# Chunked reads at the loop's opening, more steps inside the loop, and the second group's output projection moved into its last quarter

## The chip, the cores and the metric

The kernel runs on one core of a Trainium2 chip. The metric is the device time of one execution in microseconds (us). The time before is the median of three runs, 2076.06 us (2075.85 to 2076.21).

## The reference

A language-model tower on 8 sequences of 256 tokens, 2048 tokens in all, width D = 192. First comes a stack of four layers (12 heads of 16, each token attends to keys at a distance of up to 64). Then come a channel attention, a mixture of four experts, a full self-attention with 12 heads over each sequence, and a mixture of eight experts. Cut to what matters here:

```python
for l in range(4):                       # LAYERS
    q, k, v = heads(h @ Wq[l] + bq[l]), heads(h @ Wk[l] + bk[l]), heads(h @ Wv[l] + bv[l])
    a = band_attention(q, k, v, mask)    # softmax(q k^T / 4) v, |distance| <= 64
    h = layer_norm(h + a @ Wo[l] + bo[l], ln1_s[l], ln1_b[l])
    f = gelu(h @ W1[l] + b1[l])          # 192 -> 768
    h = layer_norm(h + f @ W2[l] + b2[l], ln2_s[l], ln2_b[l])
```

The later full self-attention uses the same attention code, without a band.

## The kernel before, in words

**Tiles and groups.** The 2048 tokens are 16 tiles of 128 tokens (NT), in four groups g of four tiles (GT). A group holds two of the eight sequences, called batches b in the code. The layer loop runs four times (`Fori`); the later full attention calls the same functions a fifth time. Each engine has its own instruction list, in an order that is written out by hand, and the lists meet at semaphores.

**Opening of a layer.** A tile of `h` is turned by TensorE (`pe_transpose`, L396) and split into a high and a low part by ScalarE (`act_split`, L603) and VectorE (`dve_split`, L707, L708). This is called a tile here. A group's projection has seven items: three chunks of 128 columns for q and k together (64 of each, so four heads; `pe_features`, L414 to L418; ScalarE reads the bank with `act_qk`, L621) and four v tiles (`pe_tokens`, L424 to L428; `dve_v`, L727). Each q or k value is cut into three bf16 pieces: for group 0 by VectorE (`dve_pieces`, L716 to L718), for the others by GpSimd (`pool_pieces`, L946 to L949). GpSimd cuts v as well (`pool_v`, L983 to L986). The pieces go through memory to get their layout: the SP queue writes them to `qk_rows` (L960, six DMAs a group, with runs of 1,024 bytes), waits for all six, and reads each batch back with 12 DMAs (L969) into `qx` and `kx`, in runs of 512 bytes, since a head's 16 rows lie apart from the next head's. The opening handles tiles 0 to 15, all seven items of group 0 and the three chunks of group 1. Then the loop's first scores wait for the 12 reads of batch 0.

**Loop.** A layer's 96 pairs of heads p (24 a group, 12 a batch) run as a software pipeline. For each p, TensorE makes the scores of pair p (L501 mask, L504), the value products of pair p-5 (L533 to L535) and the transposes of the probabilities of pair p-3 (L515). VectorE takes maxima (L735) and makes `ptl` (L741). ScalarE makes two exponentials (L638) and `pth` (L649). Between the pairs stand single steps which all use one PSUM bank, `BM[0]`: the items of the next group, one every third pair (`next_projection`; group 1 has only its four v tiles there, at p = 1, 4, 7, 10; groups 2 and 3 have chunks at the first three places of their 24 pairs and v tiles at the next four), and, from p = 70 in every second pair, `late_step`: four tiles of the attention output turned and split ("att", tiles 0 to 3), four output projections ("out", tiles 0 to 3, five matmuls and one addition on VectorE), then att of tiles 4 to 7.

**Tail.** After the loop TensorE projects tiles 4 to 7 (`pe_out_group(1)`), turns group 0 of the normed `h` (`pe_turn(2, 0)`) and runs the hidden layer (`pe_hidden`, L414 to L418 and L596). The turns of later groups and two more output groups stand at fixed places in it (`under`). VectorE's order is in `dve_tail`: the residual and statistics of group 1, then turn(2, 0), then for each group affine, residual, statistics and turn(2, g+1). GpSimd makes the reciprocal root (`pool_rstd`, L895, L896).

Of the kernel before, what the change touches and what calls it, by code (L numbers as in the profile page):

```python
# [24 lines left out]
ALU = mybir.AluOpType  # L25
# [7 lines left out]
B, S, D, FF = 8, 256, 192, 768  # L33
# [14 lines left out]
SLOTS = ((0, 0), (0, 1), (1, 0), (1, 1), (0, 2), (2, 0))  # L48
ROWS = DH * len(SLOTS)
ITEMS = 7  # L50
AHEAD = 3
LATE = 70
# [63 lines left out]
def build_tower(nc, a, out, stop=None):  # L116
    ctx = ExitStack()
    with ctx:
# [151 lines left out]
        pieces_out = sig("pieces_out", per=96 * NG, base=0)  # L270
        qk_in = [sig(f"qk_in_{j}", per=16 * 12 * len(range(j, B, 3)), base=0) for j in range(3)]
# [70 lines left out]
        qk_rows = [nc.dram_tensor(f"qk_rows_{j}", (2, 3, D, GW), BF16, kind="Internal").ap() for j in range(2)]  # L342
# [21 lines left out]
        def late_step(p):  # L364

            i = (p - LATE) // 2
            if p < LATE or (p - LATE) % 2 or i >= 3 * GT:
                return None
            return ("att", i) if i < GT else ("out", i - GT) if i < 2 * GT else ("att", i - GT)

        def pe_late(pe, it, p, w):

            if late_step(p) is None:
                return
            kind, t = late_step(p)
            if kind == "att":
                if t == 0:
                    pe.wait_ge(vf_ready.sem, vf_ready.at(it, 4 * NG))
                if t == GT:
                    pe.wait_ge(o_read.sem, o_read.at(it, GT))  # L380
                pe_transpose(pe, it, turned(1, t), t, xn, att_ready, it, t + 1, True)
            else:
                if t == 0:
                    pe.wait_ge(wb_ready.sem, wb_ready.at(it, 1))
                    pe.wait_ge(xx_ready.sem, xx_ready.at(it, turned(1, GT - 1) + 1))
                else:
                    pe.wait_ge(o_read.sem, o_read.at(it, t))
                pe_tokens(bank[BM[0]][:, 0:D], w, 0, D, t).then_inc(o_done.sem, 1)
# [41 lines left out]
        def projection_at(g, i):  # L430

            n = ITEMS * g + i
            return bank[BM[n % 3 if n < ITEMS + AHEAD else 0]]

        def pe_qkv(pe, it, g, i, wa):


            n = ITEMS * g + i
            proj_read(pe, it, n - (3 if n < ITEMS + AHEAD else 1))
# [7 lines left out]
        def proj_read(pe, it, n):  # L447

            g, i = n // ITEMS, n % ITEMS
            if n < 0:  # L450
                return
            if i < 3:
# [1560 lines left out]
```

## Time and profile before

| | |
|---|---|
| Median of three runs | 2076.06 us |
| Profiled execution, its own time | 2083.07 us |
| Its span, first to last instruction | 2081.2 us |
| Mean granted TensorE clock | 0.877 |
| Busy: PE, DVE, ACT, POOL | 75%, 65%, 53%, 34% of the span |
| Pairs of the second layer, first to last maximum | 151.3 us (390.76 to 542.04) |
| From its last maximum to the third layer's first | 143.69 us |

Busy shares are a mean over stages with different limits, so the stages are read apart, by stretches of the span. All times of one instruction are counted from the span's start. The chain of waits tells what ended an idle stretch; a wait for several semaphores is put down to the last. The kernel does the same in each of the four layers, and most rows below are of the second (from 352 us on).

### The profile page before, as it was taken

To read this page: it belongs to the slowest core of one execution; us is meant where nothing else is said; L and a number is where in the kernel's file an instruction comes from. 1 tells how busy PE (TensorE), PEld (TensorE's weight loads), DVE (VectorE), ACT (ScalarE), POOL (GpSimd) and SP (SyncE) were. 2 spreads that over 40 slices of the span, in tenths; PEclk is the share of its full clock that TensorE was granted. 3 is DMA by queue.
4 is the path that set the end of the run, shared out by engine and by line. 5 is a ranking of instruction groups with operands and counts; after the bars stand their busy time and mean duration, and the time that the engine had idled before them with its cause. 6 is when DMAs were issued, how large, how long until landed. Compare 5 with 4: busy or idle time off the path is not lost.

```text
span 2081.2 us, 47737 instructions
## 1 busy us (share of the span) xinstructions
PE 1567.8 (75%) x14634; PEld 1321.3 (63%) x14634; DVE 1350.8 (65%) x3622; ACT 1106.3 (53%) x3351; POOL 710.9 (34%) x989
## 2 busy tenths in 40 slices
PE   0589787798787798786898865975936887649993
PEld 0467666677576677674776663845925666449992
DVE  5688865688865789755889654243446998454444
ACT  0389732699523799324897312323515996225551
POOL 5644123534132552124441231013444340034541
PEclk9899888899898999898998885877967999669996
DMA  5868100876001955005681000015727660147775
GB/s 138 163 111 99 25 1 2 151 95 87 2 1 36 146 86 68 1 1 98 113 99 27 1 7 6 1 41 173 231 89 103 88 86 2 41 150 227 238 233 165
DMA packets 191387, 178.61 MB, mean 86 GB/s; under 512 B 23056, under 2 KB 176208, under 8 KB 190992
## 3 DMA queue, kind: packets, MB, share of 16 engines
q1 hardware_dynamic: 183824, 158.19, 39.2%
q0 software_dynamic: 7296, 17.18, 2.4%
q8 instruction: 129, 2.11, 0.5%
q14 instruction: 138, 1.13, 0.2%
HBM read 132.96 MB, written 42.34 MB: 84 GB/s over the span
## 4 chain that ended last, share of the span: by engine, by line
PE 49%; DVE 23%; issue 11%; ACT 6%; DMA 5%; POOL 2%; SPq 2%; DVEq 1%; ACTq 0%; POOLq 0%
PE bank L1313 6%; DVE ptl L741 6%; PE bank L596 5%; PE bank L515 4%; DVE neg_max L735 3%; PE bank L533 2%; PE bank L396 2%; ACT pth L649 2%; DMA kx<-qk_rows 2%; PE bank L414 2%; PE bank L1299 2%; PE bank L504 2%; ACT prob L638 2%; PE bank L417 2%; PE bank L416 2%
## 5 line engine op out<-in xcount | busy, mean ns | idle before, releaser
L638 ACT ACTIVATE prob<-bank,neg_max 128x192 f32<-128x192 f32 (+1 forms) x960 | 416.9, 438 | 71.5 <-DVE neg_max L735 40.9
L741 DVE TENSOR_TENSOR ptl<-bank,pth 128x512 f16<-128x512 f32 x480 | 329.3, 686 | 24.9 <-ACT pth L649 20.5
L735 DVE TENSOR_REDUCE neg_max<-bank 128x2 f32<-128x384 f32 (+1 forms) x480 | 274.1, 571 | 95.5 <-PE bank L504 92.4
L515 PE MATMUL bank<-ident,prob 128*128 128x128 f32 x1920 | 311.6, 286 | 0.0
L649 ACT ACTIVATE pth<-bank 128x512 f16<-128x512 f32 x480 | 286.2, 596 | 5.9 <-PE bank L515 5.8
L533 PE MATMUL bank<-v,pth 128*128 128x32 bf16 x1920 | 199.5, 180 | 114.1 <-DVE ptl L741 99.6
L533 PEld LDWEIGHTS bank<-v,pth 128*128 128x128 f16 x1920 | 154.3, 96 | 200.3 <-DVE ptl L741 193.8
L603 ACT ACTIVATE xx<-bank 128x256 fp32r<-128x256 f32 x256 | 94.7, 385 | 330.3 <-PE bank L396 325.7
L515 PEld LDWEIGHTS bank<-ident,prob 128*128 128x128 f32 x1920 | 206.6, 143 | 1.9 <-issue 1.8
L638 ACT ACTIVATION_READ_ACCUMULATOR prob<-bank,neg_max 128x1 f32 x960 | 201.2, 210 | 0.0
L535 PE MATMUL bank<-v,ptl 128*128 128x32 bf16 x1920 | 193.9, 176 | 1.3 <-issue 1.3
L534 PE MATMUL bank<-v,pth 128*128 128x16 bf16 x1920 | 190.1, 169 | 0.0
L504 PE MATMUL bank<-kx,qx 96*128 96x192 bf16 (+1 forms) x960 | 169.9, 259 | 6.5 <-DMA kx<-qk_rows 6.5
L895 POOL TENSOR_SCALAR rstd<-mv 128x4 f32<-128x4 f32 x52 | 12.0, 231 | 458.4 <-DVE mv L821 452.1
L396 PE MATMUL bank<-ident,h 128*128 128x128 f32 x256 | 56.6, 340 | 140.0 <-DVE xx L708 88.6
L534 PEld LDWEIGHTS bank<-v,pth 128*128 128x128 f16 x1920 | 157.0, 97 | 0.2
L535 PEld LDWEIGHTS bank<-v,ptl 128*128 128x128 f16 x1920 | 154.7, 96 | 0.0
L679 ACT ACTIVATE fbuf<-bank,b 128x512 f32<-128x512 f32 x96 | 65.8, 687 | 166.8 <-PE bank L418 166.7
L501 PE MATMUL bank<-mask,ident 128*128 128x384 bf16 x384 | 131.7, 343 | 24.6 <-DMA kx<-qk_rows 24.6
L596 PE MATMUL bank<-w,fbuf 128*128 128x192 f32 x768 | 146.1, 337 | 0.0
L596 PEld LDWEIGHTS bank<-w,fbuf 128*128 128x128 f32 x768 | 136.8, 198 | 8.4
L396 PE MATMUL bank<-ident,xn 128*128 128x128 f32 x256 | 57.8, 344 | 105.1 <-DVE xn L831 53.4
(274 smaller groups left out, 4233.4 us busy)
## 6 DMA issues: line engine op xcount, KB each, us to landing
xn<-in_e_seg SPq DMA_DIRECT2D x34, 768.0 KB
qx<-qk_rows SPq DMA_DIRECT2D x240, 96.0 KB, 5.1
kx<-qk_rows SPq DMA_DIRECT2D x240, 96.0 KB, 7.5
qk_rows<-fbuf SPq DMA_DIRECT2D x80, 192.0 KB, 2.8
w<-in_e_w SPq DMA_DIRECT2D x23, 576.0 KB
qk_rows<-piece_c SPq DMA_DIRECT2D x40, 192.0 KB, 3.0
hb<-in_e_w SPq DMA_DIRECT2D x11, 576.0 KB
y_rows<-mask SPq DMA_DIRECT2D x8, 768.0 KB, 8.7
```

The costliest lines, as they stand in the source:

```text
L396: last = nc.tensor.transpose(o[:, c * P:c * P + P], src[:, t, c * P:c * P + P], ident[:, :])
L501: nc.tensor.matmul(o, ident_bf, mask[:, 2 * b + qt, :].unsqueeze(1).to_broadcast([P, 2, D]), start=True, stop=False)
L504: last = nc.tensor.matmul(o[:, e, :], qx[0:ROWS, b % 3, hd + e, qt * P:qt * P + P], kx[0:ROWS, b % 3, hd + e, ks], start=not banded, stop= ...
L515: last = nc.tensor.transpose(bank[BT[p % 2]][:, (2 * e + c) * P:(2 * e + c) * P + P], prob[:, qt, hd % PROBS, c * P:c * P + P], ident[:, :])
L533: nc.tensor.matmul(o2, pth[:, p % 3, w], v[:, 0:32], start=(c == 0), stop=False)
L534: nc.tensor.matmul(o1, pth[:, p % 3, w], v[:, 32:48], start=False, stop=False)
L535: last = nc.tensor.matmul(o2, ptl[:, p % 2, w], v[:, 0:32], start=False, stop=(c == 1))
L596: last = nc.tensor.matmul(bank[BY[t]][:, 0:D], fbuf[:, (n - 2) % 4, t * P:t * P + P], w2[:, c, :], start=(c == 0), stop=(c == FC - 1))
L638: nc.scalar.activation(prob[:, qt, hd % PROBS, c0:c0 + n], scores_at(u // 2, n)[:, u % 2, :], ACT.Exp, bias=neg_max[:, tile_no % 3, hd:hd ...
L649: nc.scalar.activation(pth[:, p % 3, :], bank[BT[p % 2]][:, :], ACT.Copy).then_inc(hi_ready.sem, 1)
L735: nc.vector.tensor_reduce(neg_max[:, t % 3, hd:hd + 2], scores_at(p, D if banded else S), AX.X, ALU.max, negate=True).then_inc(max_ready.s ...
L741: nc.vector.tensor_tensor(ptl[:, p % 2, :], bank[BT[p % 2]][:, :], pth[:, p % 3, :], ALU.subtract)\
```

## The change

1. **Layout and reads.** The columns of q and k are packed on the host so that a chunk's 64 rows are ordered by row of the head first. `qk_rows` is laid out by batch and chunk, in rows of 2,048 bytes (four heads). A batch's reads become 6 DMAs of such rows, from 12. The writes are cut by batch: 12 DMAs a group with runs of 512 bytes, from 6.
2. **Opening.** For batch 0 the SP queue writes its six parts as the chunks come, then reads chunk by chunk (3 x 6 DMAs, each chunk with its own semaphore), and only then writes batch 1 and reads it. Pairs 0, 2 and 4 each wait for their own chunk. The opening turns tiles 4 to 7 only and has group 0's items only.
3. **Steps inside.** `STEPS` puts into each 24 pairs the next group's chunks at 0, 2 and 8, the tiles of the group after that at 4, 6, 10 and 12, and the v tiles at 14 to 20. `LATE` puts att of tiles 0 to 3 at p = 52, 54, 58, 60, out of 0 to 3 at 70 to 76, att of 4 to 7 at 78 to 84, and out of tiles 4 to 7 at 86 to 92. Before each step TensorE waits until the step before has been read out of the bank. The statistics of group 0 move from p = 88 to p = 80.
4. **Tail.** `pe_out_group(1)` is gone. On VectorE turn(2, 0) now comes before the statistics of group 1, and turn(2, g+1) comes right after affine, before the residual and statistics of the group before. turn(1, g+2) is moved ahead of the second affine.

```diff
-SLOTS = ((0, 0), (0, 1), (1, 0), (1, 1), (0, 2), (2, 0))
-ROWS = DH * len(SLOTS)
+SLOTS = (((0, 3), (0, 1), (0, 2)), ((0, 2), (0, 3), (0, 1)))
+READS = sum(len(s) for s in SLOTS)
+ROWS = DH * sum(n for _, n in SLOTS[0])
 ITEMS = 7
-AHEAD = 3
-LATE = 70
+STEPS = {0: ("chunk", 0), 2: ("chunk", 1), 4: ("tile", 0), 6: ("tile", 1), 8: ("chunk", 2), 10: ("tile", 2), 12: ("tile", 3),
+         14: ("v", 0), 16: ("v", 1), 18: ("v", 2), 20: ("v", 3)}
+LATE = (52, 54, 58, 60, 70, 72, 74, 76, 78, 80, 82, 84, 86, 88, 90, 92)
...
+        def step(p, banded):
+
+            g, k = p // PAIRS_G + 1, p % PAIRS_G
+            if banded and p in LATE:
+                i = LATE.index(p)
+                return ("att", "out")[i // GT % 2], i % GT + GT * (i // (2 * GT)), None
+            if g < NG and k in STEPS:
+                kind, i = STEPS[k]
+                if kind != "tile":
+                    return kind, g, i
+                if g + 1 < NG:
+                    return kind, GT * (g + 1) + i, None
+            return None
...
-            if p % (PAIRS // B) == 0:
-                pe.wait_ge(qk_in[b % 3].sem, qk_in[b % 3].at(it, 16 * 12 * (b // 3 + 1)))
+            if b == 0 and qt == 0 and hd % 4 == 0:
+                pe.wait_ge(first_in[hd // 4].sem, first_in[hd // 4].at(it, 16 * READS))
...
             def out(g):
-                dve_turn(dve, it, 1, g)
                 dve_residual(dve, ch, it, 0, g)
                 dve_stats(dve, ch, it, 0, g, o_read)
 
-            dve_residual(dve, ch, it, 0, 1)
+            dve_turn(dve, it, 2, 0)
             dve_stats(dve, ch, it, 0, 1, o_read)
-            dve_turn(dve, it, 2, 0)
             for g in range(NG + 1):
                 if g + 1 < NG:
                     dve_affine(dve, ch, it, first(g + 1), g + 1, 0)
+                    dve_turn(dve, it, 2, g + 1)
                 if g:
                     dve_residual(dve, ch, it, 1, g - 1)
                     dve_stats(dve, ch, it, 1, g - 1, y_read)
-                if g + 1 < NG:
-                    dve_turn(dve, it, 2, g + 1)
+                if g + 2 < NG:
+                    dve_turn(dve, it, 1, g + 2)
                 if g:
                     dve_affine(dve, ch, it, second(g - 1), g - 1, 1)
...
+                if g == 1:
+                    pool.wait_ge(first_out[i].sem, first_out[i].at(it, 32))
+                else:
+                    pool.wait_ge(pieces_out[0].sem, pieces_out[0].at(it, 96 * (g - 1)))
+                pool.wait_ge(pieces_out[1].sem, pieces_out[1].at(it, 96 * g))
...
-            for i in range(3):
-                if g == 0:
+            def write(b, i, done):
+                for a in range(2):
+                    dst = qk_rows[g % 2][b % 2, a, i, :, :].rearrange("(z r) (h n) -> (r h) z n", r=DH, n=S)
+                    sp.dma_start(dst, pieces[i][64 * a:64 * a + 64, :, b % 2 * S:b % 2 * S + S]).then_inc(done.sem, 16)
+
+            def read(b, chunks, done, middle=None):
+                heads = slice(4 * chunks.start, 4 * chunks.stop)
+                for a, dst in enumerate((qx, kx)):
+                    first = 0
+                    for z, n in SLOTS[a]:
+                        if middle and a == 1 and z == SLOTS[1][-1][0] and first:
+                            middle()
+                            middle = None
+                        src = qk_rows[g % 2][b % 2, a, chunks, DH * z:DH * (z + n), :].rearrange("i r n -> r i n")
+                        rows = slice(DH * first, DH * (first + n))
+                        sp.dma_start(dst[rows, b % 3, heads, :].rearrange("r (i h) n -> r i (h n)", h=4), src)\
+                            .then_inc(done.sem, 16)
...
+            if g == 0:
+                for i in range(3):
                     sp.wait_ge(first_pieces.sem, first_pieces.at(it, i + 1))
-                else:
+                    write(0, i, first_out[i])
+                for i in range(3):
+                    sp.wait_ge(first_out[i].sem, first_out[i].at(it, 32))
+                    read(0, slice(i, i + 1), first_in[i])
+                for i in range(3):
+                    write(1, i, pieces_out[1])
+                sp.wait_ge(pieces_out[1].sem, pieces_out[1].at(it, 96))
+                read(1, slice(0, 3), qk_in[1])
+            else:
+                for i in range(3):
                     sp.wait_ge(next_pieces.sem, next_pieces.at(it, 3 * (g - 1) + i + 1))
-                for a in range(2):
-                    sp.dma_start(qk_rows[g % 2][a, :, 64 * i:64 * i + 64, :].rearrange("z r n -> r z n"),
-                                 pieces[i][64 * a:64 * a + 64, :, :]).then_inc(pieces_out.sem, 16)
-            sp.wait_ge(pieces_out.sem, pieces_out.at(it, 96 * (g + 1)))
-            for b in (2 * g, 2 * g + 1):
-                if b >= 3 and b % 2:
-                    sp.wait_ge(s_done.sem, s_done.at(it, PAIRS // B * (b - 2)))
-                for a, dst in enumerate((qx, kx)):
-                    for r, slot in enumerate(SLOTS):
-                        src = qk_rows[g % 2][a, slot[a], :, b % 2 * S:b % 2 * S + S]
-                        sp.dma_start(dst[DH * r:DH * r + DH, b % 3, :, :], src.rearrange("(h r) n -> r h n", r=DH))\
-                            .then_inc(qk_in[b % 3].sem, 16)
+                    for b in range(2):
+                        write(b, i, pieces_out[b])
+                sp.wait_ge(pieces_out[0].sem, pieces_out[0].at(it, 96 * g))
+                read(2 * g, slice(0, 3), qk_in[2 * g % 3],
+                     lambda: sp.wait_ge(pieces_out[1].sem, pieces_out[1].at(it, 96 * (g + 1))))
+                sp.wait_ge(s_done.sem, s_done.at(it, PAIRS // B * (2 * g - 1)))
+                read(2 * g + 1, slice(0, 3), qk_in[(2 * g + 1) % 3])
 
...
-                pe_out_group(pe, it, wb, 1)
-                pe_turn(pe, it, 2, 0, 8)
...
-    two = [w.reshape(w.shape[:-1] + (3, 64)) for w in (q, k)]
+    two = [np.swapaxes(w.reshape(w.shape[:-1] + (3, 4, DH)), -1, -2).reshape(w.shape[:-1] + (3, 64)) for w in (q, k)]
```

The later attention (without a band) gets points 1 to 3, apart from `LATE`.

## Rows read from the trace of the kernel before

**Rows 1.** Stretch: last maximum of the second layer to the third's first.

```profile
core 0: us, PE busy (x) PEld busy (x) DVE busy (x) ACT busy (x) POOL busy (x), PEclk, DMA share, GB/s
542.04:685.73 143.69, 106.77 (x594) 91.03 (x595) 83.99 (x291) 44.18 (x89) 44.43 (x68) 0.86 0.15 21
```

**Rows 2.** Timeline of TensorE, opening of the second layer: start, duration, operation, idle before.

```profile
366.04 0.63 PE L414 MATMUL bank<-xx,wa_hi 128*128 128x512 f32 x1
...
368.18 0.47 PE L414 MATMUL bank<-xx,wa_hi 128*128 128x512 f32 x1
...
389.90 0.50 PE L501 MATMUL bank<-mask,ident 128*128 128x384 bf16 x1 [5.88 <-DMA kx<-qk_rows]
...
391.06 0.51 PE L424 MATMUL bank<-wa_hi,xx 128*128 128x192 f32 x1
...
392.23 0.54 PE L501 MATMUL bank<-mask,ident 128*128 128x384 bf16 x1
```

**Rows 3.** Timeline of the SP queue, same opening: issues of writes, then reads.

```profile
369.67 3.36 SPq L960 DMA_DIRECT2D qk_rows<-fbuf  x4
373.59 1.24 SPq L960 DMA_DIRECT2D qk_rows<-piece_c  x2
376.99 2.76 SPq L969 DMA_DIRECT2D qx<-qk_rows  x6
379.78 4.10 SPq L969 DMA_DIRECT2D kx<-qk_rows  x6
```

**Rows 4.** Stretches of the second layer: the reads, then pairs 6 to 12.

```profile
377.00:390.00 13.00, 7.07 (x37) 5.60 (x37) 4.34 (x17) 4.33 (x10) 9.56 (x18) 0.89 1.08 121
...
398.20:407.70 9.50, 9.04 (x140) 7.68 (x138) 8.11 (x18) 8.91 (x33) 5.71 (x13) 1.00 0.86 310
```

**Rows 5.** Stretches of its loop: pairs 24 to 36, then 36 to 48.

```profile
426.60:447.00 20.40, 18.77 (x253) 15.07 (x252) 17.23 (x36) 19.22 (x67) 10.89 (x13) 1.00 0.27 53
447.00:465.40 18.40, 16.30 (x244) 13.37 (x243) 16.71 (x39) 16.55 (x62) 6.91 (x16) 1.00 1.07 123
```

**Rows 6.** Stretches: pairs 0 to 6, 18 to 24, 72 to 75, 75 to 78, 78 to 81.

```profile
390.76:398.18 7.42, 7.28 (x57) 6.14 (x56) 4.96 (x10) 5.87 (x25) 6.16 (x7) 0.67 1.19 153
...
418.02:426.63 8.61, 7.56 (x117) 5.87 (x116) 7.94 (x19) 8.21 (x32) 0.00 (x0) 1.00 1.21 124
...
504.67:508.98 4.31, 3.24 (x45) 2.38 (x43) 4.31 (x13) 3.83 (x17) 0.00 (x0) 1.00 1.22 120
508.98:514.93 5.95, 5.16 (x79) 4.44 (x80) 5.36 (x13) 5.53 (x22) 1.22 (x3) 1.00 0.63 130
514.93:519.42 4.49, 3.75 (x50) 2.89 (x48) 4.49 (x12) 3.41 (x15) 2.97 (x3) 1.00 0.01 2
```

**Rows 7.** Timeline of GpSimd: first pieces of group 1, two chunks.

```profile
385.35 0.61 POOL L946 CAST fbuf<-qf 128x512 bf16<-128x512 f32 x1 [0.33 <-POOL v L986]
...
389.68 0.61 POOL L946 CAST fbuf<-qf 128x512 bf16<-128x512 f32 x1 [0.27 <-POOL fbuf L949]
```

**Rows 8.** Timeline of VectorE in the tail of the second layer.

```profile
553.30 0.35 DVE L808 TENSOR_TENSOR h<-bank,hb 128x192 f32<-128x192 f32 x1
...
556.63 1.13 DVE L817 BATCH_NORM_STATS2 stats<-h 128x6 f32<-128x192 f32 x4
...
558.01 0.29 DVE L707 TENSOR_TENSOR xx<-bank,xx 128x128 fp32r<-128x128 f32 x1
...
560.42 2.30 DVE L851 SCALAR_TENSOR_TENSOR hb<-h,mv,ln_s 128x192 f32<-128x192 f32 x4
```

**Rows 9.** GpSimd's reciprocal root there.

```profile
558.70 1.03 POOL L896 TENSOR_TENSOR rstd<-rstd,neg_half 128x4 f32<-128x4 f32 x1 [0.18 <-POOL rstd L895]
```

**Rows 10.** TensorE's idle times in that tail.

```profile
591.19 1.14 PE L396 MATMUL bank<-ident,h 128*128 128x128 f32 x4 [3.44 <-DVE xx L708]
598.36 0.89 PE L396 MATMUL bank<-ident,xn 128*128 128x128 f32 x4 [0.84 <-DVE xx L708]
617.14 1.14 PE L396 MATMUL bank<-ident,h 128*128 128x128 f32 x4 [2.65 <-DVE xx L708]
```

More of the change, by code:

```diff
@@ new lines, in pe_step @@
+        def pe_step(pe, it, p, banded, w, w_out, tile, xx):
+            if step(p, banded) is None:
+                return
+            back = [step(q, banded) for q in range(p) if step(q, banded)]
+            if not back:
+                pe.wait_ge(vf_ready.sem, vf_ready.at(it, 4))
+            else:
+                kind, a, b = back[-1]
+                if kind == "chunk":
+                    pe.wait_ge(qf_ready.sem, qf_ready.at(it, 3 * a + b + 1))
+                elif kind == "v":
+                    pe.wait_ge(vf_ready.sem, vf_ready.at(it, 4 * a + b + 1))
+                elif kind == "tile":
+                    pe.wait_ge(xx_ready.sem, xx_ready.at(*xx(a + 1)))
+                elif kind == "att":
+                    pe.wait_ge(xx_ready.sem, xx_ready.at(it, turned(1, a) + 1))
+                else:
+                    pe.wait_ge(o_read.sem, o_read.at(it, a + 1))
+            kind, a, b = step(p, banded)
+            if kind in ("chunk", "v"):
+                if b == 0:
+                    pe.wait_ge(xx_ready.sem, xx_ready.at(*xx(GT * (a + 1))))
+                pe_qkv(pe, it, a, b + 3 * (kind == "v"), w)
+            elif kind == "tile":
+                tile(a, True)
+            elif kind == "att":
+                pe_transpose(pe, it, turned(1, a), a, xn, att_ready, it, a + 1, True)
+            else:
+                if a % GT == 0:
@@ L432, in projection_at @@
             n = ITEMS * g + i
-            return bank[BM[n % 3 if n < ITEMS + AHEAD else 0]]
+            return bank[BM[n % 3 if n < ITEMS else 0]]
         def pe_qkv(pe, it, g, i, wa):
-            n = ITEMS * g + i
-            proj_read(pe, it, n - (3 if n < ITEMS + AHEAD else 1))
+            if g == 0 and i >= 3:
+                proj_read(pe, it, i - 3)
             o = projection_at(g, i)
@@ L468, in beside @@
         def beside(tile, xx=None):
-            steps = {2 + i: (lambda i=i: (tile(GT + 2 * i), tile(GT + 2 * i + 1))) for i in range((NT - GT) // 2)}
-            steps["xx"] = xx
-            return steps
+            return {2: lambda: (tile(GT), tile(GT + 1)), 4: lambda: (tile(GT + 2), tile(GT + 3)), "tile": tile, "xx": xx}
         def under(turn, out=None):
@@ L664, in act_attention @@
                     act_exp(act, it, 2 * p + 1, banded)
-                if next_projection(p):
-                    g, i = next_projection(p)
-                    if i < 3:
-                        act_qk(act, it, g, i)
-                if banded and late_step(p) and late_step(p)[0] == "att":
-                    act_split(act, it, turned(1, late_step(p)[1]), late_step(p)[1], True)
+                if step(p, banded):
+                    kind, a, b = step(p, banded)
+                    if kind == "chunk":
+                        act_qk(act, it, a, b)
+                    elif kind == "tile":
+                        split["tile"](a, True)
+                    elif kind == "att":
+                        act_split(act, it, turned(1, a), a, True)
         def act_hidden(act, it, b1, sigs, func, before):
@@ L771, in dve_attention @@
         def dve_attention(dve, ch, it, banded, split):
-            for n in range(ITEMS + AHEAD):
+            for n in range(ITEMS):
                 if n < 3:
```

122 lines of the change are left out of this document (48 added, 74 removed).

## Prediction

> **What bounds the kernel now.** I read the views in this order: the stretch between two layers' loops, the timelines of TensorE and the SP queue in an opening, the stretches of the loop by pairs, and the timelines of the tail. Between the last maximum of the second layer and the first of the third lie 143.69 us, in which ScalarE is busy for 44 [rows 1]. This time is a chain of waits, and its last link is a DMA: TensorE has finished its part of the opening and stands idle 5.88 us, until 389.90, for the reads of batch 0 [rows 2]. The last writes are issued at 373.59 + 1.24 = 374.83; the first read goes out at 376.99, 2.16 us later, since it waits for them to land [rows 3]. From 377 to 390 the DMA engines are busy all the time (share 1.08) and yet move only 121 GB/s; in pairs 6 to 12, with the weights in the queue, they move 310 [rows 4]. So the 12 reads are limited by the handling of their 512-byte runs. The loop is another regime: in pairs 24 to 36 ScalarE is busy 19.22 of 20.40 us and VectorE 17.23 [rows 5]. There nothing waits for long, and what is put in costs time.
>
> **The opening (gain).** After the change the SP queue writes batch 0 at the same moments (chunk 2 is done no earlier), so it is free at 374.83. The first chunk's pieces were written at 369.67 and have landed by then. It issues 6 reads; the rows show 2.76/6 = 0.46 us each, and 2.8 us together. The landing takes as long as that of the last write, 2.16 us, since the six move a third of a batch. The first scores come at 374.83 + 2.8 + 2.2 = 379.8 instead of 389.90 [rows 2, 3]: 10.1 us earlier, five times (four layers and the later attention, whose opening has the same order): -50.5 us. If the reads keep 121 GB/s, a third of 1.18 MB takes 3.3 us and the gain is some 9. If all five openings have SP issues as quick as the fastest, it is 11. TensorE itself is ready before 379.8: of its work up to 383.6 it loses eight tiles and three chunks. Batch 1 is late next: its writes stand behind all 18 reads, 374.83 + 18 x 0.46 = 383.1, plus 6 x 0.62 and 2.16, landed at 389.0; its reads land near 394, and pair 12 needs them some 20 us after 379.8. That is hidden by 5 us.
>
> **What is put into the loop (cost).** Six pairs without a step (18 to 24) take 8.61 us, 1.435 a pair [rows 6]. Twelve pairs with three v tiles take 18.40 instead of 17.2: 0.4 each. Twelve with three chunks and one v take 20.40: (20.4 - 17.2 - 0.4)/3 = 0.93 a chunk [rows 5]. Three pairs with two att steps take 4.31, with two out steps 4.49, against 4.3: 0 to 0.1 each; three pairs with one att take 5.95, which would be 1.6 [rows 6] but has a change of weights beside it. A tile step has just the instructions of an att step. I take 0.25 us for a tile or an out, nearer to the stretches with two of them, and keep 0 and 1.6 as ends.
>
> - Pairs 0 to 6 run at a granted clock of 0.67, that is mostly at 1.2 GHz, and TensorE is busy for 7.28 of 7.42 us [rows 6]. There a chunk costs TensorE its own time, 368.18 - 366.04 = 2.14 us by the second chunk of the opening, and ScalarE and VectorE have air. Two chunks enter (4.3), two v tiles leave (392.23 - 391.06 = 1.17 and, at the higher clock, some 0.6) [rows 2]: +2.5, and +0.25 for the tile at p = 4.
> - Pairs 6 to 24: one chunk 0.93, three tiles 0.75, and two more v tiles than now 0.8: +2.5.
> - Pairs 24 to 48: four tiles: +1.0. Pairs 48 to 96: four outs: +1.0; the att steps only change places.
> - GpSimd: it may cut group 1 only once batch 1's writes have landed, at 389.0 instead of 385.35, and a chunk takes it 4.33 us [rows 7]. The third chunk's read on ScalarE (p = 8) waits for the first one's pieces, done at 393.3. ScalarE comes there near 379.8 + 10.4 + 2.75 = 393. I put 0.5 us for it, with 0 and 3 as ends; behind that read stand the next pair's exponentials, and with them the whole pipeline.
>
> A layer pays 2.75 + 2.5 + 1.0 + 1.0 + 0.5 = 7.75, the later attention (no outs) 6.75: 4 x 7.75 + 6.75 = +37.75 us.
>
> **The tail (gain).** `pe_out_group(1)` goes, so turn(2, 0) begins at 553.3 on VectorE instead of 558.01. But what the hidden layer needs two steps on is the affine of group 1, and this waits for statistics. Now: statistics 556.63 to 558.01, GpSimd's root until 558.70 + 1.03 = 559.73, affine at 560.42 behind turn(2, 0) [rows 8, 9]. After: turn(2, 0) 553.3 + 2.4 = 555.7, statistics until 557.1, root until 558.8, affine at 558.8. Of the 4.3 us that the hidden layer starts earlier only 1.6 stay. The new order on VectorE takes the residual and statistics from in front of turns (2, 2) and (2, 3): the waits of 3.44 and 2.65 us should come down to the 0.84 of an undisturbed turn [rows 10], 2.6 + 1.8 = 4.4. The residual that comes later instead frees the banks for the next products while TensorE makes a feature step, so I see no new wait. Together 6.0 a layer, four times: -24 us. The ends are 2 (the waits move to the banks) and 8.5 (the whole early start stays).
>
> **Sum.** -50.5 + 37.75 - 24 = -36.75 us. The profiled execution took 2083.07 (a span of 2081.2 and 1.9 around it), 7.0 above the median of the runs. On it the sum gives 2046.3; on the median of 2076.06, 2039.3. I say 2039.
>
> **A rule against it.** In the Trainium skill, DMA: Bandwidth & Descriptors, section Specifications, 512 bytes are the least size for moving data at line rate, so by this rule longer runs bring nothing to a read. Rows 4 speak against the rule here: 121 GB/s with 512-byte runs and 310 with longer ones. What would follow if it held is rival 2.
>
> **Rivals.**
> 1. *The SP queue and GpSimd become the wait.* If an issue takes 0.6 us rather than 0.46, batch 1's writes land 2.5 us later, pieces come at 396 and ScalarE stands at p = 8 for some 3 us in each of five loops. For it: 18 small issues stand ahead. Against: GpSimd idles later, so nothing else shifts. 2039 + 5 x 2.5 = 2052.
> 2. *Run length is not the limit of reads.* They stay at 121 GB/s. The first chunk comes 1 us later, the third at about 387 when pair 4 wants it at 386, batch 1 at about 401 against a need at 400: 2 us a loop, 2049.
> 3. *The steps cost much more (slower).* All steps use one bank, and TensorE waits for each before the next; its list also holds the score and value products that ScalarE and VectorE live on. 40 tiles and 16 outs at the 1.6 us of rows 6 instead of 0.25 add 76 us: 2115. The sign turns where the extra is 36.75/56 = 0.66, so at 0.9 us a step. Against: att steps in every second pair, with the same bank and waits, show 0 to 0.1.
> 4. *More stays.* The whole early start of the tail stays (+2.5 a layer), tiles and outs are free (14 us), and the first chunks run at 2.4 GHz, as the idle time ahead of the loop is shorter (1 us a loop): 2039 - 10 - 14 - 5 = 2010; with half of it, 2024.
> 5. *The early reads do nothing*, as something else holds the first scores, such as the v tiles of group 0. Against: their last read by VectorE is done before 380. Only costs and the tail are left: 2076 + 38 - 24 = 2090.
>
> **How the numbers follow.** The forecast, 2028 to 2047: 0.50. More stays, below 2028: 0.18. Rivals 1 and 2, 2047 to 2062: 0.18. Costlier steps short of the turn, 2062 to 2072: 0.04. Rivals 3 and 5 past it: 0.07, and 0.03 within 0.2% (4 us), which is about what a measurement of this kernel can tell from no change. So faster 0.90, same 0.03, slower 0.07. The range of 8 in 10 runs from 2020 to 2062.
>
> **What the changed profile would show.** The first scores 5.0 us after the last write of batch 0 is issued, and no wait of 5.9 us for `kx`. From the last maximum of the second layer to the first of the third about 127.6 us instead of 143.7 (10.1 and 6.0 less). The first six pairs near 10.2 us, pairs 0 to 95 near 159 instead of 151.3. Turns (2, 2) and (2, 3) without waits over 1 us. The prediction is wrong if the loop grows by over 12 us a layer (steps), if a long wait for GpSimd's pieces stands before L621, or if scores wait for a DMA at p = 12.

## The result, and the profile after

| | before | after |
|---|---|---|
| Median, same chip | 2076.01 us (4 runs, 2075.85 to 2076.21) | 2026.18 us (4 runs, 2024.22 to 2031.86) |
| Ratio, 95% interval | | 0.9764 [0.9745, 0.9784] |
| Profiled execution, span | 2083.07, 2081.2 us | 2031.86, 2030.0 us |
| Mean granted TensorE clock | 0.877 | 0.884 |

The change makes the kernel 49.8 us faster on the medians. The forecast was 2039, 13 us too high, in the range of 2020 to 2062. The profiled executions, 51.2 us apart, are split at the first and last maximum (L750 after) of each loop:

| us, layers 1 to 4, then the later attention | before | after | difference |
|---|---|---|---|
| start of the span to the first maximum | 93.52 | 81.51 | -12.0 |
| loops (pairs 0 to 95) | 153.0, 151.3, 150.9, 151.5, 146.1 | 159.5, 160.0, 159.4, 160.1, 151.1 | +37.3 |
| last maximum to the next loop's first, layers 1 to 3 | 144.2, 143.7, 142.5 | 126.4, 126.6, 124.9 | -52.5 |
| the same behind layer 4 (channel attention and experts lie between) | 464.8 | 439.1 | -25.6 |
| behind the last loop | 339.8 | 341.4 | +1.6 |

All rows are again of the second layer, whose first maximum now is at 367.36. **The stretch of [rows 1]** is 17 us shorter; TensorE is busy in it for 11 us less and GpSimd for 12, since steps moved into the loop. The second line is the stretch of the first reads, from their first issue to the maximum of pair 5 (columns as in [rows 1]):

```profile
527.39:654.03 126.64, 95.92 (x543) 80.61 (x544) 81.94 (x270) 39.22 (x78) 32.55 (x55) 0.86 0.05 11
362.20:375.50 13.30, 10.46 (x49) 7.69 (x47) 5.01 (x13) 6.08 (x22) 7.15 (x16) 0.62 0.55 133
```

**The opening**, as [rows 2, 3] show it before. TensorE first, then the SP queue:

```profile
366.50 0.50 PE L516 MATMUL bank<-mask,ident 128*128 128x384 bf16 x1 [2.31 <-DMA kx<-qk_rows]
367.03 0.78 PE L440 MATMUL bank<-xx,wa_hi 128*128 128x512 f32 x1
369.31 0.54 PE L516 MATMUL bank<-mask,ident 128*128 128x384 bf16 x1
...
370.52 0.78 PE L440 MATMUL bank<-xx,wa_hi 128*128 128x512 f32 x1
```

```profile
360.84 1.23 SPq L970 DMA_DIRECT2D qk_rows<-piece_c  x2
362.20 1.45 SPq L982 DMA_DIRECT2D qx<-qk_rows  x3
363.69 1.35 SPq L982 DMA_DIRECT2D kx<-qk_rows  x3
...
369.27 1.35 SPq L982 DMA_DIRECT2D kx<-qk_rows  x3
370.66 3.64 SPq L970 DMA_DIRECT2D qk_rows<-fbuf  x4
```

The last write of batch 0 is issued at 362.07, and the first read 0.13 us later. The first scores come at 366.50, 4.4 us after that write, where [rows 2, 3] had 15.07: 10.6 us gained. The six reads of a chunk are issued in 2.8 us, as forecast, and the landing takes 1.5. During the reads the DMA engines are busy for 0.55 of the time, against 1.08 in [rows 4]: now the queue's issues set the pace, not the engines. Each of the chunks at p = 0 and p = 2 (from L440 on) takes 2.1 to 2.3 us on TensorE; the granted clock of the stretch is 0.62, so mostly 1.2 GHz.

**The loop**, against [rows 5, 6]: pairs 0 to 6, 6 to 12, 24 to 36 and 36 to 48. Pairs 72 to 75, which now hold two outs, take 4.41 us.

```profile
367.36:377.36 10.00, 8.96 (x64) 6.54 (x64) 5.01 (x11) 7.36 (x26) 3.58 (x8) 0.75 0.55 122
377.36:388.61 11.25, 10.34 (x141) 8.09 (x137) 9.39 (x19) 10.67 (x40) 9.10 (x11) 1.00 0.94 247
406.84:430.41 23.57, 20.04 (x258) 15.60 (x257) 21.03 (x42) 20.04 (x72) 16.67 (x16) 1.00 0.27 55
430.41:448.63 18.22, 16.24 (x242) 13.41 (x243) 17.30 (x41) 16.29 (x60) 7.25 (x16) 1.00 0.75 154
```

Pairs 24 to 36 grew by 3.2 us, and VectorE is busy for 3.8 us more in them. That is more than the tiles in them explain, and the next rows tell why. They are of GpSimd and of VectorE at pair 25:

```profile
408.59 2.22 POOL L943 TENSOR_TENSOR wb_lo<-raw,wb_hi 128x960 fp32r<-128x960 f32 x1 [0.18 <-POOL wb_second L941]
410.77 2.36 POOL L944 TENSOR_TENSOR wb_second_lo<-raw,wb_second 64x960 fp32r<-64x960 f32 x1
```

```profile
409.94 1.09 DVE L782 TENSOR_TENSOR xn<-au,rs 128x192 f32<-128x192 f32 x1
410.95 2.26 DVE L783 TENSOR_TENSOR xn<-au,rs 128x64 f32<-128x64 f32 x1
```

L783 takes 0.22 us elsewhere (median of 80). Here it ends only when GpSimd's L944 does. The weights stand in GpSimd's list where they stood, behind the last v tile of group 1, and this tile has moved from p = 10 to p = 20. So GpSimd comes to them at pairs 24 to 27, no longer at 12 to 18. It is the steps that do it: with the old reads (experiment 2) pairs 24 to 27 take the same 7.36 us. The collision itself is old. In the kernel before, VectorE's norm met the two casts of the same weights, and took 2.1 us instead of 0.57:

```profile
410.00 1.11 DVE L767 TENSOR_TENSOR xn<-au,rs 128x192 f32<-128x192 f32 x1
411.04 1.00 DVE L768 TENSOR_TENSOR xn<-au,rs 128x64 f32<-128x64 f32 x1
```

```profile
409.92 0.98 POOL L931 CAST wb_hi<-raw 128x960 fp32r<-128x960 f32 x1 [0.26 <-POOL v L986]
410.84 1.12 POOL L932 CAST wb_second<-raw 128x960 fp32r<-128x960 f32 x1
```

GpSimd's pieces of group 1 do start later in the loop, 10 us behind the first maximum, where they started 5.4 us ahead of it:

```profile
377.44 0.61 POOL L959 CAST fbuf<-qf 128x512 bf16<-128x512 f32 x1 [5.19 <-DMA qk_rows<-piece_c]
...
381.84 0.61 POOL L959 CAST fbuf<-qf 128x512 bf16<-128x512 f32 x1 [0.34 <-POOL fbuf L962]
```

These answer to [rows 7]: a chunk takes 4.40 us, and the first waits for batch 1's writes, landed 15 us after the last write of batch 0 (14 were forecast).

**The tail**, against [rows 8 to 10]: VectorE and GpSimd, then the two turns of `h` for groups 2 and 3.

```profile
541.30 1.13 DVE L827 BATCH_NORM_STATS2 stats<-h 128x6 f32<-128x192 f32 x4
...
544.44 2.75 DVE L861 SCALAR_TENSOR_TENSOR hb<-h,mv,ln_s 128x192 f32<-128x192 f32 x4 [1.68 <-POOL rstd L905]
```

```profile
575.16 0.89 PE L422 MATMUL bank<-ident,h 128*128 128x128 f32 x4 [0.99 <-DVE xx L723]
...
597.25 0.89 PE L422 MATMUL bank<-ident,h 128*128 128x128 f32 x4 [0.84 <-DVE xx L723]
```

The affine of group 1 begins 17.05 us after the last maximum, where it was 18.38: 1.3 us of the earlier start stay. The waits of 3.44 and 2.65 us are 0.99 and 0.84.

### The profile page after: what moved, and what is told of

The parts are those of the page before. It is cut to its first block, busy times and chain, and to the rows that moved or that the text cites. A ratio compares the mean times of both kernels' runs of the same rounds, so it can differ in the third digit from the quotient of the medians.

```text
span 2030.0 us, 47816 instructions
## 1 busy us (share of the span) xinstructions
PE 1550.0 (76%) x14634; PEld 1298.0 (64%) x14634; DVE 1359.3 (67%) x3622; ACT 1104.2 (54%) x3351; POOL 711.3 (35%) x989
## 4 chain that ended last, share of the span: by engine, by line
PE 45%; DVE 23%; issue 12%; ACT 10%; DMA 4%; POOL 3%; SPq 2%; DVEq 1%; ACTq 0%; POOLq 0%
PE bank L1349 7%; PE bank L605 5%; DVE ptl L756 4%; ACT prob L647 4%; PE bank L530 4%; ACT pth L658 4%; DVE neg_max L750 2%; DVE h L870 2%; PE bank L422 2%; PE bank L548 2%; PE bank L1335 2%; PE bank L440 1%; ACT xx L612 1%; DVE xx L723 1%; DVE xn L841 1%
## 5 line engine op out<-in xcount | busy, mean ns | idle before, releaser
L750 DVE TENSOR_REDUCE neg_max<-bank 128x2 f32<-128x384 f32 (+1 forms) x480 | 274.1, 571 | 81.7 <-PE bank L519 80.7
L605 PEld LDWEIGHTS bank<-w,fbuf 128*128 128x128 f32 x768 | 132.5, 194 | 12.6 <-issue 5.3
```

The source lines that it names most:

```text
L605: last = nc.tensor.matmul(bank[BY[t]][:, 0:D], fbuf[:, (n - 2) % 4, t * P:t * P + P], w2[:, c, :], start=(c == 0), stop=(c == FC - 1))
L750: nc.vector.tensor_reduce(neg_max[:, t % 3, hd:hd + 2], scores_at(p, D if banded else S), AX.X, ALU.max, negate=True).then_inc(max_ready.s ...
```

## The experiments

Each run has its ratio to the kernel before, timed on the same chip. "The changed kernel" is the one the diff shows. Run again it gave 0.9751 [0.9722, 0.978] (`after_again`, 2031.79 us).

One thing bears on several of them. Behind the channel attention, up to the first router, 78 products of TensorE stand that no edit touches. In ten of the traces, both of the changed kernel and the one before among them, they take 33.4 to 34.1 us. In four (`reads_only`, `wait_all`, `short_runs`, `chunk_open`) they take 41.6, at a granted clock of 0.50. First `after_again`, then `wait_all`:

```profile
1326.69:1360.37 33.68, 22.58 (x78) 9.57 (x78) 16.41 (x74) 9.23 (x25) 5.20 (x8) 0.70 0.18 63
```

```profile
1342.46:1384.05 41.59, 31.09 (x78) 11.21 (x78) 16.41 (x74) 9.89 (x25) 5.19 (x8) 0.50 0.14 51
```

So 7.9 us of what the traces of these four lose say nothing of their edits. One execution of each was profiled; whether all of them have it is not shown.

**1. The reads alone** (`reads_only`): layout and chunked reads, with the steps and the tail of before. The diff is against the changed kernel; the rest of what goes back (`step` and the tail) is not shown.

```diff
-LATE = (52, 54, 58, 60, 70, 72, 74, 76, 78, 80, 82, 84, 86, 88, 90, 92)
+AHEAD = 3
+LATE = 70
...
```

> The kernel before with the new layout, the chunked reads and their semaphores, and its old schedule of steps. TensorE is busy with tiles 8 to 15 and group 1's chunks until 383.6 in the second layer, so the first scores can come near 384 and no longer wait for a DMA: 389.9 - 384 = 6 us a loop, 30 us in all, less what a later batch 1 costs. Theory (the gain of the opening needs both the early reads and the emptied opening): about 2046. Rival (the reads alone carry the gain of 10.6 us an opening, as the tiles are hidden): about 2023. Rival (the reads were not the wait): 2076.

2101.24 us, 1.0124 [1.0082, 1.0166]: slower than before, by 27 us. The first scores do come early (383.7 instead of 389.9, and the loop's start with them), but pairs 0 to 6 take 18.7 us instead of 7.4. ScalarE, then GpSimd, in its second layer:

```profile
383.07 0.78 ACT L626 ACTIVATE qf<-bank,bqk,q_scale 128x512 f32<-128x512 f32 x1 [0.58 <-PE bank L421]
...
394.26 0.78 ACT L626 ACTIVATE qf<-bank,bqk,q_scale 128x512 f32<-128x512 f32 x1 [10.41 <-POOL fbuf L958]
```

```profile
390.18 0.61 POOL L955 CAST fbuf<-qf 128x512 bf16<-128x512 f32 x1 [5.42 <-DMA qk_rows<-piece_c]
```

The third chunk of group 1 is still ahead of the loop in ScalarE's list. It wants a `qf` slot that GpSimd frees, and GpSimd waits until batch 1 is written, which now comes behind 18 reads. This is the mechanism of rival 1, with 10.4 us a layer where I had put 3. In the whole change it is absent, because the third chunk is a step at p = 8. My expectation, which priced the reads without it, was wrong.

**2. The steps and the tail alone** (`steps_only`): the changed kernel with the old layout and reads.

```diff
-            if b == 0 and qt == 0 and hd % 4 == 0:
-                pe.wait_ge(first_in[hd // 4].sem, first_in[hd // 4].at(it, 16 * READS))
+            if p % (PAIRS // B) == 0:
+                pe.wait_ge(qk_in[b % 3].sem, qk_in[b % 3].at(it, 16 * 12 * (b // 3 + 1)))
...
```

> The changed kernel with the old layout and the 12 unchunked reads of a batch. The first scores go back to 15.1 us after the last write of batch 0, and steps cost what they cost, while the tail keeps its gain. Theory (costs 38 us, tail gains 24): about 2076 + 14 = 2090, at least 50 us over the changed kernel. Rival (the loop's early steps were hidden in the opening's idle time before, so they cost less when the loop starts late): 2076 to 2080.

2074.77 us, 1.0006 [0.9991, 1.0021]: no change. Loops are 6.5 to 7.1 us longer (4.6 in the later attention), the stretches between the four layers' loops 6.9 to 9.3 us shorter. So the two roughly cancel. My 2090 was 15 us too high: the five loops cost 31.5 us where I had 37.75, and I had put the tail at 6.0. The time is the rival's, but its reason is not borne out: pairs 0 to 6 of the second layer cost 9.9 us with the late start, and 10.0 with the early one. The difference from here to the whole change is what layout and reads bring once the steps are in: 1.0006 less 0.9764, 0.0242 of 2076 or 50 us. The traces put it in the openings: the start and the four stretches between loops are 50.4 us shorter in the changed kernel. The forecast for the openings was 50.5.

**3. VectorE's old order in the tail** (`tail_old`).

```diff
                     dve_affine(dve, ch, it, first(g + 1), g + 1, 0)
-                    dve_turn(dve, it, 2, g + 1)
                 if g:
                     dve_residual(dve, ch, it, 1, g - 1)
                     dve_stats(dve, ch, it, 1, g - 1, y_read)
+                if g + 1 < NG:
+                    dve_turn(dve, it, 2, g + 1)
```

> The changed kernel with one part undone: VectorE does turn(2, g+1) of the hidden layer after the residual and statistics of the group before, as it used to. Theory: waits of 3.4 and 2.7 us come back in front of turns (2, 2) and (2, 3), 4.4 us a layer, +17.6 us: about 2044. Rival (the time was given back at the banks, where the next products wait for a later residual): no change, 2026.

2051.56 us, 0.9899 [0.986, 0.9938]; its four runs lie between 2040.56 and 2062.73. The waits in front of the turns (2, 2) and (2, 3) are back:

```profile
577.29 0.89 PE L422 MATMUL bank<-ident,h 128*128 128x128 f32 x4 [3.44 <-DVE xx L723]
...
601.23 0.89 PE L422 MATMUL bank<-ident,h 128*128 128x128 f32 x4 [3.17 <-DVE xx L723]
```

The stretches between loops grow by 4.5, 3.8, 7.7 and 4.3 us. The order is worth some 20 us or more, where the forecast gave it 17.6 (4.4 a layer).

**4. Group 1's output projection back in the tail** (`out1_tail`).

```diff
-LATE = (52, 54, 58, 60, 70, 72, 74, 76, 78, 80, 82, 84, 86, 88, 90, 92)
+LATE = (52, 54, 58, 60, 70, 72, 74, 76, 78, 80, 82, 84)
...
+            dve_residual(dve, ch, it, 0, 1)
+            dve_stats(dve, ch, it, 0, 1, o_read)
             dve_turn(dve, it, 2, 0)
-            dve_stats(dve, ch, it, 0, 1, o_read)
...
-                pe_turn(pe, it, 2, 0, None)
+                pe_out_group(pe, it, wb, 1)
+                pe_turn(pe, it, 2, 0, 8)
```

> The changed kernel with the output projection of tiles 4 to 7 back behind the loop, ahead of turn(2, 0). Prediction: it costs 1.6 us a layer in the tail, gives back 1.0 in the loop: +2.4 us in all, 2028. Rival (the whole earlier start of the hidden layer stays, 4.3 a layer): +13 us, 2039. Rival (the four steps in the loop are dearer, 0.9 us each): about 8 us faster, 2018.

2022.73 us, 0.9747 [0.9725, 0.9769], against 0.9764 [0.9745, 0.9784]. The intervals overlap: the part that stands last in the change's name, the projection in the last quarter, is worth nothing that can be measured. Pairs 80 to 95 take 23.2 us without its four outs and 23.8 with them. The forecast had given it 0.6 us a layer.

**5. All three chunks awaited at pair 0** (`wait_all`).

```diff
-            if b == 0 and qt == 0 and hd % 4 == 0:
-                pe.wait_ge(first_in[hd // 4].sem, first_in[hd // 4].at(it, 16 * READS))
+            if p == 0:
+                for i in range(3):
+                    pe.wait_ge(first_in[i].sem, first_in[i].at(it, 16 * READS))
```

> The changed kernel with pair 0 waiting for all three chunks of batch 0 instead of its own. The last of the 18 reads is issued 5.6 us after the sixth, so the first scores come 5.6 us later; pairs 4 and 5 lose nothing by it. Theory: 5.6 us a loop, +28 us, about 2054. Rival (the start-up is limited by the chunk put at p = 0 and p = 2, so half of it is caught up): +14, 2040.

2058.88 us, 0.9872 [0.9847, 0.9898]: 27 us more than the changed kernel on that chip. TensorE's first scores in the second layer:

```profile
376.12 0.48 PE L517 MATMUL bank<-mask,ident 128*128 128x384 bf16 x1 [7.58 <-DMA kx<-qk_rows]
```

The idle time is 7.58 us instead of 2.3, 5.3 more, and five openings make 26 us of it. In the traces (against `after_again`) start and openings are 26 us longer, the loops 4 shorter, and the 7.9 of the stretch behind the channel attention come on top. Without these the 27 us are some 19, below the theory's 28 and above the rival's 14.

**6. The first batch in short runs** (`short_runs`): batch 0 goes through rows padded by 64 bytes between heads, so that a run is 512 bytes again; DMAs, order and waits stay.

```diff
+        qk_first = nc.dram_tensor("qk_first", (2, 3, 3 * DH, 4, S + 32), BF16, kind="Internal").ap()
...
+                        if b == 0:
+                            src = qk_first[a, chunks.start, DH * z:DH * (z + n), :, 0:S]
+                            sp.dma_start(dst[rows, b % 3, heads, :], src).then_inc(done.sem, 16)
```

> The changed kernel with the rows of batch 0 padded in memory by 64 bytes a head, so that its reads move in runs of 512 bytes instead of 2,048, with the same DMAs, order and waits. Theory (run length is what limited the reads, 121 GB/s): a chunk of 0.39 MB takes 3.3 us of the DMA engines against 2.8 us of issue, so the first scores come 1 us later, the third chunk 2 us, and batch 1 later by 2: +5 to +10 us in all. Rival (run length doesn't matter): no change in the distance of 4.4 us from the end of the writes to the first scores.

2049.67 us, 0.9831 [0.9806, 0.9856]: 17.9 us more than the changed kernel on that chip. In its trace 7.9 of it lie in the stretch behind the channel attention. What is left, 10, is at the upper end of the expected 5 to 10, and the traces have 7.6 of it in the first six pairs of the five loops. The SP queue tells why:

```profile
365.65 1.87 SPq L987 DMA_DIRECT2D qx<-qk_first  x3
```

An issue takes 0.63 us, 0.45 with the long runs, and all 18 take 11.5 us instead of 8.4. The first scores come 5.8 us after the last write (4.4 in the changed kernel), and at pair 4 they wait another 2.07 us for the third chunk. The DMA engines are busy for under half of the time, in the stretch of these 18 issues:

```profile
365.65:377.20 11.55, 8.11 (x37) 5.84 (x36) 3.48 (x11) 3.94 (x16) 7.13 (x16) 0.59 0.46 107
```

So this edit costs through the time of an issue, and not, as the forecast had it, through the rate of the engines. It does not show that run length sets that time: in the kernel before, six reads with runs of 512 bytes too were issued in 2.76 us, 0.46 each [rows 3]. Nor does run length alone explain the engines' share: 107 GB/s of 512-byte runs here are 0.46 of it, and 121 GB/s in [rows 4] are 1.08. Padding, the rows per DMA and the number of reads waiting in the queue differ as well, and no run takes them apart. Experiments 5 and 6, without their 7.9 us, give 19 and 10 us of the 50 of experiment 2 (an estimate; they were not undone together). The rest belongs to what neither undoes: six reads a batch instead of twelve, and batch 0's reads ahead of batch 1's writes.

**7. The chunk of p = 0 ahead of the loop** (`chunk_open`), in TensorE's idle time before the first scores.

```diff
+                if p == 0:
+                    return None
...
+            pe.wait_ge(vf_ready.sem, vf_ready.at(it, 2))
+            pe_qkv(pe, it, 1, 0, w)
             for p in range(PAIRS + 5):
```

> The changed kernel with one step moved: the first chunk of group 1 goes from p = 0 to the end of the opening, into the 2.3 us in which TensorE waits for the first reads, with a bank of its own. In the loop it costs TensorE 2.1 us at 1.2 GHz between the scores of pairs 0 and 1. Theory: pairs 0 to 6 take 7.9 us instead of 10.0 and the first scores come at the same time: about 10 us faster than the changed kernel, 2016. Rival (ScalarE's and VectorE's start-up sets these six pairs, the chunk is hidden there): no change.

2033.77 us, 0.9759 [0.9729, 0.9789], against 0.9751 for the changed kernel: nothing. With 7.9 us behind the channel attention in its trace, the time alone would not settle it, but the first six pairs do: over the five loops they take 48.7 us, and 48.9 in `after_again`. The chunk's 2 us are free in the opening, but pair 2 wants the second chunk of reads, and that comes when it came:

```profile
366.67 0.48 PE L518 MATMUL bank<-mask,ident 128*128 128x384 bf16 x1 [2.05 <-DMA kx<-qk_rows]
```

Reads issued at 2.8 us a chunk allow two pairs in 2.8 us. The chunk at p = 0 was hidden behind them.

**8. The weights of the tail, cut** (`weights_cut`): GpSimd's L943 and L944 in quarters of 240 columns. **With out1 in the tail** as well: `weights_cut_out1`.

```diff
+                for s in range(0, c1, c1 // 4):
+                    e = s + c1 // 4
+                    nc.gpsimd.tensor_tensor(lo[:, s:e], raw[:, 0, s:e], hi[:, s:e].bitcast(F32), ALU.subtract)
...
```

> The changed kernel, with GpSimd's two long subtractions for the low part of the tail's weights (L943 2.22 us and L944 2.36 us, over 960 columns) each cut into four of 240 columns. Theory A, two-tensor operations with both inputs in SBUF take turns on VectorE and GpSimd: after the change L943 and L944 lie at pairs 24 to 26 where VectorE norms an attention tile, and its L782 and L783 take 1.09 and 2.26 us instead of 0.35 and 0.22, 2.8 us together. With quarters VectorE waits for 0.6 us at most before it gets its turn: L783 at most 0.9 us, pairs 24 to 27 fall from 7.36 us towards the 5.77 of the later attention (which has no such weights there), 1.4 to 1.6 us a layer, some 6 us in all: a ratio to before near 0.973 instead of 0.976. Theory B, the two operations are slow for another reason (the tile step or the chunk beside them): pairs 24 to 27 stay at 7.36 and L783 at 2.26. Theory C, VectorE never gets its turn between back-to-back operations of GpSimd: L783 stays above 2 us and nothing is won.

> The same cut in the variant in which group 1's output projection stays in the tail, which measured 0.9747 [0.9725, 0.9769] on another chip. If the cut is worth 6 us and the place of the projection nothing, this comes out at the same ratio as the other kernel of this pair, near 0.972, and both lie below the changed kernel. If the projection in the loop does bring the 2.4 us a layer that the forecast gave it once the weights no longer hold VectorE, this one is some 10 us slower than the other, 0.977.

2027.41 us, 0.9741 [0.972, 0.9762], and 2024.4 us, 0.9737 [0.9712, 0.9762]. Pairs 24 to 27 and 27 to 36 of the second layer, first of `after_again`, then of `weights_cut`:

```profile
408.14:415.51 7.37, 5.56 (x56) 4.09 (x54) 6.62 (x11) 4.57 (x18) 7.01 (x6) 1.00 0.32 68
415.51:431.71 16.20, 14.37 (x203) 11.49 (x203) 14.40 (x32) 15.46 (x56) 9.66 (x11) 1.00 0.24 50
```

```profile
404.42:410.16 5.74, 5.57 (x57) 4.11 (x55) 4.93 (x11) 4.71 (x18) 5.56 (x8) 1.00 0.34 64
410.16:427.53 17.37, 14.56 (x203) 11.44 (x203) 15.72 (x31) 15.21 (x55) 12.19 (x15) 1.00 0.23 47
```

The first stretch fell by 1.6 us, to what the later attention shows (5.77), in all four layers alike, so theory A holds there. But 1.17 us come back in the second: the next norm of VectorE now meets a subtraction of GpSimd's pieces. VectorE, then GpSimd:

```profile
419.08 1.19 DVE L783 TENSOR_TENSOR xn<-au,rs 128x64 f32<-128x64 f32 x1
```

```profile
418.82 1.37 POOL L971 TENSOR_TENSOR fbuf<-qf,fbuf 128x512 bf16<-128x512 f32 x1 [0.18 <-POOL fbuf L970]
```

What stays is 0.5 us a layer, too little for the timing to show. The place of the projection again makes no difference. (The expectation misquotes the forecast: that gave the projection 0.6 us a layer, 2.4 in all.)

**9. The same weights, later** (`weights_later`, and `weights_later_out1`): GpSimd handles them behind the pieces of group 2.

```diff
+                pool_pieces(pool, ch, it, 2)
                 pool.wait_ge(rows_y.sem, rows_y.at(it, 16 * 8))
                 alone(pool)
                 pool_weights(ch, wb, SEG).then_inc(wb_ready.sem, 1)
-                pool_pieces(pool, ch, it, 2)
```

> The changed kernel, with GpSimd's four operations on the tail's weights (6.6 us) moved from before its pieces of group 2 (pairs 24 to 28) to behind them. There GpSimd has 5.5 us of idle time before the first v tile of group 2 (5.1 us in which no step feeds it), and VectorE norms its next tile at the very start of that stretch. Theory A (turns of two-tensor operations, and the late chunks behind them): pairs 24 to 27 fall from 7.36 to about 5.8 us as in the later attention, pairs 27 to 36 from 16.2 to 15.5, and pairs 36 to 48 keep their 18.2 or gain at most 0.6: 1.7 to 2.4 us a layer, 7 to 10 in all, a ratio near 0.971. Unlike the kernel with the cut operations nothing is given back at the norm near pair 32, since the pieces come 6.6 us earlier. Theory B, the collision moves with them: L783 shows 2 us or more at pair 37, and the sum of pairs 24 to 48 stays at 41.8.

> The same move in the variant with group 1's output projection in the tail. It should match the other kernel of this pair within 3 us (the place of the projection was worth nothing in two pairs of runs); if it is 8 us or more off, the projection's place matters after all.

2034.07 us, 0.9796 [0.9783, 0.981], and 2039.0 us, 0.9805 [0.9781, 0.9828]. Pairs 24 to 36 fall from 23.6 to 21.4 us, as theory A said, but pairs 36 to 42 rise from 9.4 to 14.6. This is theory B, and worse than it had it. VectorE's norm at 430.88, then the stretches from 430.9 to 434.5, to 437.8 and to 442.68:

```profile
430.88 1.54 DVE L782 TENSOR_TENSOR xn<-au,rs 128x192 f32<-128x192 f32 x1
432.34 2.22 DVE L783 TENSOR_TENSOR xn<-au,rs 128x64 f32<-128x64 f32 x1
```

```profile
430.90:434.50 3.60, 1.42 (x15) 1.12 (x12) 3.60 (x4) 0.77 (x3) 3.58 (x2) 1.00 0.84 182
434.50:437.80 3.30, 2.12 (x27) 1.87 (x28) 2.55 (x6) 1.98 (x8) 0.34 (x1) 0.51 1.04 194
437.80:442.68 4.88, 4.88 (x59) 4.47 (x55) 3.10 (x8) 3.07 (x11) 1.78 (x4) 0.63 1.06 190
```

Two operations of 0.57 us take 3.76. TensorE runs dry meanwhile (3.36 us idle before its next value product), and afterwards its granted clock is 0.51 and 0.63 for 8 us. So 3.2 us of waiting become 5.2 us of loop.

None of the variants beats the changed kernel by more than the intervals allow: the lowest ratios, 0.9737, 0.9741 and 0.9747, all overlap its 0.9764 and 0.9751.

## Why the prediction was right, and what it had wrong

- **The opening** (10.1 us forecast): right, 10.6 in the second layer and 11.2 in the later attention. The dissection of it was right too, 2.8 us of issues and a landing, though the landing took 1.5 and not 2.2. The reason given for the reads' slowness does not stand: "the 12 reads are limited by the handling of their 512-byte runs" fits the share of 1.08 in [rows 4], but runs of the same length need a share of 0.46 for 107 GB/s in experiment 6. What made the 12 reads slow is open. The forecast did not need it: its 10.1 us are made of issues and one landing. What rival 2 foresaw did not come: no chunk is awaited at pair 4, and the queue reads faster (133 GB/s over their stretch) with the engines half idle. The rule against it, that longer runs bring nothing, is not settled either way: short runs cost some 10 us here, by their issues. Rival 5, that the early reads do nothing, falls by experiments 2 and 5.
- **The order of the parts**: the forecast added opening and steps as if each stood alone. Experiment 1 shows that they do not. Early reads without the moved chunk lose 27 us, with it they win 50. The mechanism stood in rival 1, but I asked only what it costs in the whole change (0.5 us; there ScalarE in fact never waits for GpSimd's pieces).
- **The loop** (37.75 forecast, 37.3 measured): the sum is right, its parts less so. In the second layer pairs 0 to 6 pay 2.6 us (2.75 forecast). Pairs 6 to 24 pay 1.0 instead of 2.5 + 0.5. There was no wait for GpSimd, and the weights, which held VectorE here before, left this stretch; in the later attention, which has no such weights, these pairs pay 2.4. Pairs 24 to 48 pay 3.0 instead of 1.0: 1.6 of it is VectorE held by these same weights (experiments 8 and 9), which the forecast had not seen, because it asked who waits for GpSimd and not whom GpSimd meets. The last half pays 2.1 instead of 1.0, with 1.2 in pairs 60 to 63, where the granted clock is 0.70. Tiles are as cheap as taken: in the later attention four of them add 1.0 us to pairs 24 to 48, 0.25 each. Rival 3 is out. That the errors of the parts cancel to within 0.5 us is luck.
- **The tail** (6.0 a layer forecast): some 7. The whole stretch gives 17.1 to 17.9 us, less 10.6 of opening; by itself (experiment 2) 6.9 to 9.3. Of the early start 1.3 us stay (1.6 forecast); the hidden layer's first products come 4.5 us earlier, but wait for the same affine. The two turns gave 2.45 + 1.81 = 4.3 of the forecast 4.4.
- **The step that was off** is the sum of openings and tails: -74.5 forecast, and -90.1 + 1.6 (behind the last loop) = -88.5 measured. The first opening gave 1.9 us more than forecast, the three next stretches 4.2 more together, the one behind layer 4 9.5 more. Of that stretch's 25.6 us, 7.9 are the tail and 11.2 the opening; 3.7 fall in the channel attention and 4.7 in the first experts, neither of which the change touches, and 1.8 are given back. One stretch of the channel attention, before and then after:

```profile
1286.14:1304.74 18.60, 14.61 (x66) 12.99 (x67) 3.55 (x14) 5.04 (x11) 1.98 (x2) 0.60 0.00 0
```

```profile
1246.08:1260.98 14.90, 10.93 (x66) 9.97 (x67) 3.55 (x14) 5.04 (x11) 1.99 (x2) 0.85 0.00 1
```

The same 66 products, at 0.60 of the full clock and at 0.85. No edit touches them, and their time differs from trace to trace: 17.2 us in experiment 3, 18.4 in `weights_later_out1`, 15 in all others but the kernel before; the stretch behind them takes some 34 or 41.6 us. This is a size that no sum over edits gives. Whether every execution before has the low clock is open, since only one was profiled. Of the 4.7 us in the experts only some remain in the second run of the changed kernel, where that part took 97.6 us (99.0 before, 94.3 after). The forecast's own case "more stays", 2010 to 2028 at 0.18, is where the result fell, by tail and clock and not by free steps. Without the 3.7 and 4.7 us the profiled executions would lie 43 us apart (an estimate), against 37 forecast. So of the 14 us that the forecast lacks on them, 8.4 are no merit of the change, and the rest is a cheaper tail and opening.

## What to carry to other kernels

A wait removed at an opening is worth what the next thing in each list allows: try the edit alone in the mind, list by list, and look for an item that stands ahead of the loop and needs a buffer freed late (in experiment 1 the reads that win 50 us lost 27). Reads that a loop can take up piece by piece should come first in the queue, each with its own semaphore, and work put between their pairs can be hidden behind the issues (here the chunk at p = 0, experiment 7). Before a few us are read out of a total, look at stretches that the edit does not touch (7.9 us in four of the runs here). When an engine's list slides, ask not only who waits for it, but what it now runs beside.

## What the runs showed of the hardware

- VectorE's two-tensor operations on SBUF and GpSimd's operations there exclude each other. L783 took 0.22 us as a rule, 2.26 us beside L944 (2.36 us), 1.19 us beside a piece of 1.37 us, and 0.7 us beside quarters. GpSimd's need not have two inputs: beside the casts L931 and L932 of the kernel before, the norm's 0.35 and 0.22 us were 1.11 and 1.00. The Trainium skill says so (SBUF — State Buffer, "SBUF: two separate sides"): the pair of ports is locked for a whole instruction when VectorE has two inputs in SBUF. The traces agree. VectorE's `ptl` and tile splits, of whose two inputs one is in PSUM, kept their 0.67 and 0.29 us next to the same operations.
- Issues of one queue differ: 0.45 us a read with 2,048-byte runs and 0.63 with padded 512-byte ones, but 0.46 for the first six reads of 512-byte runs in the kernel before. Writes of batch 1 took 0.64 to 0.91 on the mean of a group.
- The share of the DMA engines does not follow from bytes and run length: 512-byte runs moved at 121 GB/s with a share of 1.08 in the kernel before, and at 107 GB/s with 0.46 in experiment 6.
- The same 78 products and what stands between them took 33.7 us at a mean granted clock of 0.70, and 41.6 at 0.50.
- 3.4 us without work on TensorE inside the loop were followed by 8 us at a granted clock of 0.51 to 0.63 (experiment 9), while 1.55 us of idle time at the same collision in the changed kernel (its pair 25) left it at 1.00.
